# The experts' products with the weights as the stationary operand: the hidden layer comes out turned, without transposes

## What is computed

```python
logits = t @ Wg                                  # t: 1024 tokens of 128
probs = jax.nn.softmax(logits, axis=-1)
top_v, top_i = jax.lax.top_k(probs, TOP_K)       # 2 of 8 experts for each token
...
for e in range(E):
    h = jax.nn.silu(t @ W1[e]) * (t @ W3[e])     # 128 -> 512
    out = out + comb[:, e:e + 1] * (h @ W2[e])   # 512 -> 128
```

## Time and profile before

| | |
|---|---|
| median of 3 runs | 442.28 us (438.8 to 443.53) |
| profiled execution | 441.79 us, of which the span of instructions is 440.0 us |
| PE busy in the span | 381.7 us (87%) |
| DVE, ACT, POOL busy | 326.9, 241.4, 201.3 us |
| granted PE clock, mean | 0.944 |
| experts, first address instruction to last Silu | 344.1 to 425.5 us |

### The profile page before, as it was taken

How to read it: one execution, slowest core, us unless ns; L and a number is a source line. 1 busy time by engine, 2 the same in 40 slices (tenths; PEclk the granted TensorE clock), 3 DMA queues, 4 the chain that set the end, 5 groups by cost and what they waited for, 6 DMA issues and landing times.

```text
span 440.0 us, 8296 instructions
## 1 busy us (share of the span) xinstructions
PE 381.7 (87%) x2779; PEld 223.3 (51%) x2779; DVE 326.9 (74%) x677; ACT 241.4 (55%) x473; POOL 201.3 (46%) x259
## 2 busy tenths in 40 slices
PE   7657799999779968997799889998799889999990
PEld 3414454575356625654544454454355465677660
DVE  5765775667776788888789899889974477676765
ACT  3713455655826471547457858766478644566551
POOL 5034898717363775357052307647141004206661
PEclk9965999999989988998899999999899999999996
DMA  7572717207301802523014203622013001411113
GB/s 188 123 193 52 161 31 165 51 1 176 77 1 37 218 0 62 131 76 117 25 55 119 79 1 109 143 73 73 6 34 103 1 13 43 123 50 49 49 49 97
DMA packets 43406, 34.70 MB, mean 79 GB/s; under 512 B 5901, under 2 KB 39757, under 8 KB 43069
## 3 DMA queue, kind: packets, MB, share of 16 engines
q1 hardware_dynamic: 42117, 31.60, 28.1%
q0 software_dynamic: 1248, 2.57, 1.8%
HBM read 15.13 MB, written 7.89 MB: 52 GB/s over the span
## 4 chain that ended last, share of the span: by engine, by line
PE 56%; DVE 20%; POOL 7%; issue 5%; ACT 5%; SPq 4%; DMA 3%; POOLq 0%; DVEq 0%; ACTq 0%
PE p_sc L630 8%; PE p_o L662 6%; PE p_misc L600 6%; PE p_misc L531 5%; DVE mx L909 5%; PE p_o L649 4%; SPq L1500 4%; PE p_misc L811 4%; PE p_sc L811 4%; PE p_misc L830 3%; PE p_o L822 3%; PE p_misc L704 2%; DVE xn L879 2%; DMA region<-qx 2%; POOL kS L1369 2%
## 5 line engine op out<-in xcount | busy, mean ns | idle before, releaser
L1249 ACT ACTIVATE probs<-p_sc 128x512 f32<-128x512 f32 x192 | 104.6, 597 | 73.8 <-PE p_sc L630 73.1
L909 DVE TENSOR_REDUCE mx<-p_misc 128x1 f32<-128x512 f32 x192 | 121.9, 683 | 16.2 <-PE p_misc L600 15.0
L1363 POOL TENSOR_SCALAR veps<-meanvar 128x2 f32<-128x2 f32 x16 | 3.7, 230 | 101.0 <-DVE meanvar L865 100.7
L600 PE MATMUL p_misc<-kS,qS 96*128 96x512 f16 x128 | 39.9, 387 | 5.4 <-DVE mx L909 5.3
L1405 POOL TENSOR_TENSOR psums<-probs 128x256 f32<-128x256 f32 x32 | 24.4, 763 | 39.7 <-PE p_o L656 35.8
L662 PE MATMUL p_o<-probs,v 128*32 128x256 f32 x512 | 41.6, 402 | 0.6 <-ACT probs L1249 0.6
L630 PE MATMUL p_sc<-qS,kS 128*128 128x256 f16 x256 | 41.2, 281 | 0.3
L649 PE MATMUL p_o<-probs,v 128*64 128x256 f32 x256 | 35.6, 400 | 3.4 <-ACT probs L1249 3.4
L1151 DVE TENSOR_TENSOR probs<-probs,p_sc 128x512 f32<-128x512 f32 x30 | 20.6, 685 | 22.8 <-ACT probs L1327 22.5
L630 PE MATMUL p_sc<-region 128*128 128x256 f16 x256 | 35.4, 284 | 2.2 <-DVE region L923 2.2
L1327 ACT ACTIVATE probs<-p_misc 128x512 f32<-128x512 f32 x30 | 17.9, 597 | 31.5 <-PE p_sc L811 31.5
(11 more groups left out here) (221 smaller groups left out, 763.7 us busy)
## 6 DMA issues: line engine op xcount, KB each, us to landing
region<-kx SPq DMA_DIRECT2D x24, 256.0 KB, 3.9
v<-in_L_ffn_W_dram SPq DMA_DIRECT2D x24, 256.0 KB, 2.7
region<-qx SPq DMA_DIRECT2D x24, 128.0 KB, 3.8
kS<-kS SPq DMA_DIRECT2D x1, 1664.0 KB
kS<-k_scratch SPq DMA_DIRECT2D x8, 192.0 KB
k_scratch<-kx SPq DMA_DIRECT2D x4, 256.0 KB, 2.8
slots_in<-qS SPq DMA_DIRECT2D x1, 975.0 KB, 10.0
slots_in<-qS SPq DMA_DIRECT2D x1, 960.0 KB, 6.0
```

Of the source, the lines that this page charges most:

```text
L600: pe.matmul(ps, q[:, i * P:(i + 1) * P], k, start=True, stop=True).then_inc(full, 1)
L909: dve.tensor_reduce(mx[:, b % 2, i, h:h + 1], ps, AX_X, ALU.max).then_inc(free, 1)
L1249: act.activation(probs[:, h % 8, half * 512:(half + 1) * 512], p_sc[:, half, :], ACT.Exp, scale=(DH0 if layer == 0 else DH1) ** -0.5).then ...
```

## The change

The operands of the first product change places: the weights are stationary, in four blocks of 128 columns each, and the 128 tokens stream. The result is the hidden layer with its index on the partitions. `hidden_t` goes, with its semaphore; `product` writes straight to `p_o`, and `high` and `low` read it there. `high` stands close behind the Silu of its own tile (k + 0.3). `down` stands at k + 2.1 and has twelve matmuls of 128 columns that all add up in the same 128 columns; `result` is then one copy on ACT, and its part on DVE goes. Beside this the numbers in `PLACES`, `SHIFTED` and `REST` are new (some 300 of them, two lines shown).

```diff
-    0: {"max": (-4.62, 1.13), "sum": 1.39, "av": (2.76, 1.36), "f_ln": 7.78, "f_xn": -8.15, "f_xT": -1.23,
+    0: {"max": (-4.87, 0.99), "sum": 1.3, "av": (3.85, 0.92), "f_ln": 8.47, "f_xn": -8.04, "f_xT": 0.36,
...
-        placed += [(k, ("gu", k)), (k + 1.3, ("hT", k)), (k + 2.6, ("dn", k))]
+        placed += [(k, ("gu", k)), (k + 0.3, ("hT", k)), (k + 2.1, ("dn", k))]
...
                 for ps, w in ((p_misc, ew[0]), (p_sc, ew[1])):
-                    for i, (ws, xs) in enumerate(((0, 0), (0, 1), (1, 0))):
-                        last = pe.matmul(ps[:, k % 2, :], takenT[half][:, xs, at], w[:, bass.ds(chosen[k], 1), ws, :].rearrange("p e n -> p (e n)"),
-                                         start=(i == 0), stop=(i == 2))
+                    for f in range(FF):
+                        block = slice(f * P, (f + 1) * P)
+                        for i, (ws, xs) in enumerate(((0, 0), (0, 1), (1, 0))):
+                            last = pe.matmul(ps[:, k % 2, block], w[:, bass.ds(chosen[k], 1), ws, block].rearrange("p e n -> p (e n)"),
+                                             takenT[half][:, xs, at], start=(i == 0), stop=(i == 2))
                 last.then_inc(gu_full, 1)
-
-            def hidden_t(k):
-                pe.wait_ge(hp_done, k + 1)
-                if k == 0:
-                    pe.wait_ge(o_free, 6 * B)
-                if k >= 2:
-                    pe.wait_ge(hl_done, k - 1)
-                for f in range(FF):
-                    last = pe.transpose(p_o[:, k % 2, f * P:(f + 1) * P], hp[:, k % 2, f * P:(f + 1) * P], ident[:, :])
-                last.then_inc(hT_full, 1)
 
             def down(k):
                 pe.wait_ge(hl_done, k + 1)
                 ps, full = misc_take(pe, ("ym", k))
-                for f in range(FF):
-                    w = ew2[:, bass.ds(chosen[k], 1), f, :, :].rearrange("p e s n -> p (e s n)")
-                    pe.matmul(ps[:, 0:2 * P], hh[:, k % 2, 0, f * P:(f + 1) * P], w, start=(f == 0), stop=False)
-                for f in range(FF):
-                    w = ew2[:, bass.ds(chosen[k], 1), f, 0, :].rearrange("p e n -> p (e n)")
-                    last = pe.matmul(ps[:, 0:P], hh[:, k % 2, 1, f * P:(f + 1) * P], w, start=False, stop=(f == FF - 1))
+                for hs, ws in ((0, 0), (0, 1), (1, 0)):
+                    for f in range(FF):
+                        w = ew2[:, bass.ds(chosen[k], 1), f, ws, :].rearrange("p e n -> p (e n)")
+                        last = pe.matmul(ps[:, 0:P], hh[:, k % 2, hs, f * P:(f + 1) * P], w,
+                                         start=(hs == ws == f == 0), stop=(hs == 1 and f == FF - 1))
                 last.then_inc(full, 1)
...
             def product(k):
                 dve.wait_ge(sg_done, k + 1)
+                if k == 0:
+                    dve.wait_ge(o_free, 6 * B)
                 if k >= 2:
-                    dve.wait_ge(hT_full, k - 1)
-                dve.tensor_tensor(hp[:, k % 2, :], sg[:, k % 2, :], p_sc[:, k % 2, :], ALU.mult).then_inc(hp_done, 1)
+                    dve.wait_ge(hh_done, k - 1)
+                dve.tensor_tensor(p_o[:, k % 2, :], sg[:, k % 2, :], p_sc[:, k % 2, :], ALU.mult).then_inc(hp_done, 1)
...
             def high(k):
-                act.wait_ge(hT_full, k + 1)
+                act.wait_ge(hp_done, k + 1)
...
             def result(k):
-                ps, _free = misc_wait(act, ("ym", k))
-                if k >= 2:
-                    misc_done(act, ("ym", k - 2))
-                act.copy(y_low[:, k % 2, :], ps[:, P:2 * P]).then_inc(y_half, 1)
+                if 4 <= k < SLOTS + 4:
+                    act.wait_ge(y_kept[k % 4], 16 * (k // 4))
+                elif k >= 4:
+                    act.wait_ge(y_sent[k % 4], 16 * sent_of(k - 4))
+                ps, free = misc_wait(act, ("ym", k))
+                act.copy(y_sb[:, k % 4, :], ps[:, 0:P]).then_inc(free, 1)
```

More of the change, by code:

```diff
@@ L78 @@
[L78 to L82, removed]
@@ L106 @@
-    (5, 'logits'): (4.57, 1.56), (5, 'max'): (2.22, 1.14), (5, 'nodes'): 4.91, (5, 'oT'): (-0.41, 1.49),
-    (5, 'oT1'): (3.4, 1.43), (5, 'place'): 20.85, (5, 'q1'): 12.67, (5, 'q1_ln'): 6.8, (5, 'q1_xT'): 11.2,
-    (5, 'q1_xn'): 9.96, (5, 'rank'): 10.48, (5, 'round'): 2.45, (5, 'route'): 12.73, (5, 'rows'): 1.38,
-    (5, 'sT'): -5.5, (5, 'send'): 10.6, (5, 'shares'): 4.61, (5, 'slope'): 4.93, (5, 'split'): (0.78, 2.24),
-    (5, 'stack'): -8.2, (5, 'stage'): (-1.47, 2.13), (5, 'up0'): (2.12, 0.29), (5, 'v1'): 6.14,
@@ L116 @@
-    (6, 'k1'): 5.74, (6, 'logits'): (10.56, 1.25), (6, 'max'): (3.51, 1.26), (6, 'nodes'): -12.77,
-    (6, 'oT'): (9.36, 2.42), (6, 'oT1'): (5.29, 0.4), (6, 'place'): 15.05, (6, 'q1'): -4.01, (6, 'q1_ln'): 8.43,
-    (6, 'q1_xT'): 8.06, (6, 'q1_xn'): 13.98, (6, 'rank'): 13.35, (6, 'round'): -7.01, (6, 'route'): 11.83,
-    (6, 'rows'): 2.88, (6, 'sT'): -6.41, (6, 'send'): 21.24, (6, 'shares'): 13.9, (6, 'slope'): 2.81,
-    (6, 'split'): (0.76, 1.9), (6, 'stack'): -25.07, (6, 'stage'): (1.91, 2.25), (6, 'up0'): (-3.67, 0.22),
@@ L131 @@
[L131 to L139 removed]
+    (0, 'aT'): (4.27, 0.05), (0, 'av'): (-0.45, 0.6), (0, 'bounce'): 1.73, (0, 'down0'): -3.31, (0, 'f_ln'): -8.73,
@@ new lines @@
+    (4, 'rank'): 13.1, (4, 'round'): 3.78, (4, 'route'): 2.05, (4, 'rows'): 4.05, (4, 'sT'): 3.55,
+    (4, 'send'): 19.67, (4, 'shares'): 17.27, (4, 'slope'): 5.84, (4, 'split'): (2.95, 1.2), (4, 'stack'): -3.04,
+    (4, 'stage'): (0.67, 1.64), (4, 'up0'): (3.08, 0.42), (4, 'v1'): 5.59, (4, 'weights'): 20.33,
+    (4, 'y0'): (6.3, 2.96), (4, 'y1'): -5.38, (5, 'aT'): (-10.57, 1.21), (5, 'aT1'): 5.35, (5, 'av'): (0.27, 1.06),
+    (5, 'best'): 19.69, (5, 'bounce'): 10.27, (5, 'compare'): 8.93, (5, 'consts'): 3.83, (5, 'count'): 18.53,
@@ new lines @@
+    (5, 'q1_xn'): 8.96, (5, 'rank'): 10.48, (5, 'round'): 2.45, (5, 'route'): 4.86, (5, 'rows'): 1.46,
+    (5, 'sT'): -5.76, (5, 'send'): 10.6, (5, 'shares'): 4.75, (5, 'slope'): 4.93, (5, 'split'): (0.64, 2.24),
+    (5, 'stack'): -10.18, (5, 'stage'): (-3.79, 2.4), (5, 'up0'): (2.12, 0.29), (5, 'v1'): 6.32,
+    (5, 'weights'): 12.13, (5, 'y0'): (13.47, 3.01), (5, 'y1'): 16.07, (6, 'aT'): (10.81, 1.64), (6, 'aT1'): 6.96,
+    (6, 'av'): (1.48, 0.73), (6, 'best'): 22.24, (6, 'bounce'): 4.86, (6, 'compare'): 13.17, (6, 'consts'): 3.82,
@@ new lines @@
+    (6, 'q1_xT'): 8.06, (6, 'q1_xn'): 13.22, (6, 'rank'): 13.64, (6, 'round'): -9.47, (6, 'route'): 12.79,
+    (6, 'rows'): 2.88, (6, 'sT'): -6.29, (6, 'send'): 21.24, (6, 'shares'): 19.3, (6, 'slope'): 3.34,
+    (6, 'split'): (0.76, 1.9), (6, 'stack'): -26.04, (6, 'stage'): (1.91, 1.83), (6, 'up0'): (-3.66, 0.16),
+    (6, 'v1'): 4.11, (6, 'weights'): 28.88, (6, 'y0'): (-1.47, 4.04), (6, 'y1'): 8.62, (7, 'aT'): (-18.57, 0.59),
+    (7, 'aT1'): 7.17, (7, 'av'): (0.39, 1.18), (7, 'best'): 28.87, (7, 'bounce'): 24.47, (7, 'compare'): 19.56,
@@ new lines @@
+    (7, 'place'): 20.76, (7, 'q1'): 14.24, (7, 'q1_ln'): 13.8, (7, 'q1_xT'): 16.93, (7, 'q1_xn'): 19.72,
+    (7, 'rank'): 8.8, (7, 'round'): -7.97, (7, 'route'): 6.28, (7, 'rows'): 6.56, (7, 'sT'): -11.53,
+    (7, 'send'): 39.58, (7, 'shares'): 7.02, (7, 'slope'): 14.87, (7, 'split'): (-2.0, 2.1), (7, 'stack'): 10.59,
+    (7, 'stage'): (0.92, 1.73), (7, 'up0'): (1.25, 0.64), (7, 'v1'): -2.14, (7, 'weights'): 15.62,
+    (7, 'y0'): (-4.34, 1.85), (7, 'y1'): 9.76}
+REST = [(0.0, 'oT1', 3, 0), (0.15, 'oT1', 3, 1), (1.05, 'aT1', 3), (1.17, 'h1', 3), (1.42, 'y1', 3),
+        (1.86, 'ln', 'ex', 3), (2.1, 'xn', 'ex', 3), (3.11, 'xT', 'ex', 3), (3.17, 'logits', 3),
+        (3.88, 'compare', 1), (4.15, 'rank', 1), (4.48, 'count', 1), (4.83, 'place', 1), (8.62, 'send', 1),
+        (10.45, 'fetch', 1), (13.17, 'gT', 1, 0), (16.0, 'dest'), (17.12, 'gT', 1, 1), (20.07, 'gT', 1, 2),
+        (23.14, 'gT', 1, 3), (31.53, 'route', 1), (36.34, 'shares', 1), (44.81, 'best', 1), (49.07, 'weights', 1)]
```

131 lines of the change are left out of this document (55 added, 76 removed), and 32 rows, old and new, of tables (PLACES, SHIFTED).

## The result

The changed kernel takes 478.23 us (median of 4, 477.81 to 480.26), the kernel before 441.80 beside it (median of 4). The ratio is 1.084, 95% interval 1.077 to 1.091: 36 us slower. The profiled execution took 480.26 us with a span of 478.4, against 441.8 and 440.0 before, so the two traces have 38.4 us between them.

A forecast was written before the change was run, and what follows sets the result against it. The array bounded the kernel before (2.39 us a tile); PE's sequencer would bound the changed one at 3.80. Tiles +30.4, last tile +0.7, tail -0.5, batch 3 +1.5 make +32.1 on 442.3: 474 us, range 458 to 485.

The forecast's parts named there:

- The bound: PE's array bounds the kernel before at 2.39 us a tile; the changed tile's array work would be 2.05 us.
- The price of an address: In PE's sequencer, each of 24 address instructions a tile takes 0.1275 us (bounds 0.123 and 0.157), 3.06 in all.
- Once a tile: PE's sequencer adds 0.64 us around loading the expert's number and 0.10 for one semaphore, giving 3.80 us a tile.
- The first tiles: Batch 3's small steps (`oT1` to `logits`) wait less behind longer first products, but semaphores stop the sequencer: +1.5 us.
- The last tile and the tail: Last tile's `gate_up` to Silu takes 2.35 us instead of 1.64 (+0.7); behind the last Silu, -0.5 us.
- The tables: New tables move steps of the attention part past each other: 0, with 4 us to either side.
- The other engines: ACT (1.45 us a tile) and DVE (1.37) fit in 3.8; the chain after `gate_up`, about 2.9 us, is hidden.
- The sum: Tiles 30.4, last tile 0.7, tail -0.5, batch 3 1.5: +32.1 us on 442.3, giving 474 us.
- Hidden addresses: Rival: PE's sequencer works ahead while the array is fed from its queue; kernel faster, 432 us; chance 0.10.
- Slow short matmuls: Rival: the array is slower than 0.057 us in an unbroken stream; at 0.081, 458 us; chance 0.03.
- Long spacing of 0.157: Rival: address instructions are 0.157 us apart as a rule; tile 4.5 us, time 494 us; chance 0.03.
- The clock fell: Rival: the granted clock falls because the array pauses; at 1.2 GHz at most 9 us more, 483; chance 0.08.

The follow-up runs named there:

- the run with eight addresses: The changed kernel with a fixed expert in the first product only, leaving eight address instructions a tile in the second: 437.0 us, ratio 0.993.
- The last kernel above: The changed kernel with two addresses per instruction, no bounds check, and the second product as in the kernel before: 434.13 us, ratio 0.987.

## Why the prediction was right, point by point

- **The bound.** Right. The array's tile is 2.01 us where nothing else bounds it (2.05 forecast), and it bounded the kernel before: taking 0.3 us of sequencer work from that one changed nothing.
- **The price of an address.** Right and a little low. 0.1305 us on average, against the chosen 0.1275 between bounds of 0.123 and 0.157. None are closer than 124 ns, and a few in a tile are farther apart, up to 0.28. The forecast's rows gave the bounds; the choice between them was a judgement, and it came out 3 ns low. Over 24 it is 3.13 instead of 3.06.
- **Once a tile.** 0.66 for the load (0.64 forecast) and 0.14 for semaphores (0.10, one; now and then there is a second). Together with the line above a tile is 3.93, not 3.80, and 29 tiles give 3.8 us more. The tile was mis-sized by 3%.
- **The first tiles.** This is the step that was mis-sized most. Over 29 paces of 3.93 us (114.0) the stretch from the first address of the first tile (342.7) to that of the last (462.0) holds 119.4, a surplus of 5.4 where the sum has +1.5. The text let the sequencer's stock of work and the longer first products swallow the waits of batch 3's small steps. They did not: the period with `oT1` to `y1` took 7.49 us, as it had 7.62 before, and with no address at all 8.12. A fall of the clock made two of these steps 1.6 us longer, which is shown below. One wait is new, and I had said that the routing gets more room and costs nothing:

```profile
PE p_misc L770 <- DVE kx L1062: 1.5, 1, 1.5
PE p_misc L811 <- DVE p_o L1142: 5.2, 15, 0.5
PEld p_misc L811 <- issue: 11.4, 24, 0.7
```

  The first row is the waits of PE from 344 to 460 us, with the time in all, how often, and the longest: PE's count of the ranks stands 1.5 us for DVE. The other two are the pace itself under its two names. The 1.6 of the clock and the 1.5 of this wait can explain at most 3.1 of the surplus of 5.4; the rest is not assigned.
- **The last tile and the tail.** Right. The first address at 462.0, the Silu at 464.31: 2.3 us (2.35 forecast). The sign named for it, a last Silu near 457, was missed by 7 us, by the tiles and the first tiles. From there to the last scatter 5.0 us, where I had 4.8:

```profile
464.31 0.60 ACT L1309 ACTIVATE probs<-p_misc 128x512 f32<-128x512 f32 x1 [1.65 <-PE p_sc L811]
```
```profile
469.31 2.23 DMA token_rows<-probs,kx
```

  The first row is of the timeline, the second of the chain that ended last, to set beside the earlier trace rows.
- **The tables.** Taken at 0 with 4 to either side: attention ends 1.4 us sooner in the profiled run, and the run with the old tables gives the same median. The 1.4 are not the tables' doing, for with the old ones it ended at 340.9, sooner still; whose they are is open.
- **The other engines.** Right. `high` on its own tile's product, two buffers and the product in PSUM show no wait of their own; without addresses the same chain ran in tiles of 2.01 (median). One sign was off: ACT was to wait over 2 us for PE ahead of each Silu, and it waits 1.73 and 1.65.
- **The sum.** In the two traces: tiles +34.2 (114.0 - 79.8), surplus +5.4, last tile and tail +0.3, attention -1.4, together 38.5 for a difference of 38.4. The forecast had 32.1. Of the 6.4 between them 3.8 are the tile, 3.9 the first tiles and -1.4 attention. The medians are 4 us apart (478.2 and 474), closer than the traces, because the profiled execution of the changed kernel is 2 us above its median. Only the 1.4 of attention went the other way; the two large misses add.
- **The rivals.** Hidden addresses: refuted, by 45 us between the changed kernel and the one without them; the 432 us named for it are what that kernel measures. The Trainium skill, "Advanced Engine Details and Errata", section on the sequencer loop, has other engine instructions read and queued while a control instruction runs in microcode. In the run with eight addresses the array does work on from its queue beside them, and the queue also runs dry. Slow short matmuls: refuted. Long spacing of 0.157: refuted. The clock fell, but for two short times and not for the stage; see below.

## What to carry to other kernels

Count the instructions that only PE's sequencer carries out (addresses by a register, value loads, semaphores) beside the matmuls, and work out a second pace from them: a matmul of 128 columns with a register address of its own costs 0.13 us, not 0.056, so cutting a product into short pieces or letting the dynamic operand be the one that changes most often is only free with fixed addresses. The average of the two paces is not enough: 17 short matmuls, 0.95 us, are all that the array had in stock here, and a longer piece of address work is felt. Busy shares do not show this bound; weight loads that wait for "issue" and even spacings above the array's do. Where it binds, pack addresses (two cost 0.15 instead of 0.26), drop the check of a loaded value that the program itself keeps in bounds, and keep dynamic operands wide.

## What was not expected of the hardware

**At half the clock, the tile was no slower.** Behind attention the granted clock falls to 0.50 at times, which it did not before. The stretches ahead of a fall, of the steps of batch 3 in it, and of one whole tile in the next (load to load 3.85 us):

```profile
345.00:352.00 7.00, 5.15 (x40) 3.66 (x38) 2.80 (x7) 3.76 (x7) 0.00 (x0) 0.86 0.00 0
352.50:356.50 4.00, 4.00 (x29) 3.94 (x30) 2.28 (x7) 0.40 (x1) 0.07 (x1) 0.50 0.01 4
367.30:371.10 3.80, 3.42 (x37) 3.24 (x38) 3.14 (x16) 0.29 (x1) 0.49 (x1) 0.50 0.00 0
```

PE was busy 5.15 of 7 us ahead of the first fall, and waited 1.5 us for DVE just ahead of the tile in the second. Why it fell is open: the kernel before was busy 4.97 of the same 7 us and kept 1.00, and the run without any address instruction fell to 0.50 as well (349 to 355 us). The array's rows of that tile:

```profile
368.03 1.46 PE L811 MATMUL p_misc<-kS,region 128*128 128x128 f16 x12 [0.38 <-issue]
369.29 1.49 PE L811 MATMUL p_sc<-kS,region 128*128 128x128 f16 x12
```

At a granted 1.2 GHz that tile took 3.85 us, like all the others. From 369.29 to the start of the second product at 370.57 twelve matmuls take 1.28 us, 0.107 each, so 36 are 3.84 us (the forecast's estimate was 4.1). Two bounds meet there, this and the sequencer's 3.93, and the fall costs next to nothing at this pace. From 383 us on the clock was 1.00, with PE's gaps in every tile.

The first fall did cost something, in the small steps of batch 3, which the addresses do not pace. The same two steps in the changed kernel, and in the kernel before at a clock of 1.00:

```profile
349.73 1.81 PE L744 MATMUL p_misc<-aT,f1w 128*128 128x256 f32 x4 [0.46 <-ACT aT L1176]
352.47 2.08 PE L752 MATMUL p_misc<-f1w,ssb 128*128 128x128 f32 x8 [0.93 <-ACT ssb L1289]
```
```profile
350.47 1.13 PE L746 MATMUL p_misc<-aT,f1w 128*128 128x256 f32 x4
352.53 1.16 PE L754 MATMUL p_misc<-f1w,ssb 128*128 128x128 f32 x8 [0.93 <-ACT ssb L1307]
```

From the start of the first to the end of the second it is 4.82 us at the fall and 3.22 without: 1.6 us. The last kernel above, whose clock fell only later, has the 3.22 again.

**An instruction of 46 ns that takes 130.** The busy time of a register instruction does not give its price, and the number of its operations hardly does: six of them are 74 ns long and come every 0.153 us, three 46 ns and every 0.1305. What fills the time between them no run shows.
